# Graph network layer on one Trainium2 core: VectorE prepares masks and one-hots further ahead, TensorE's counts move between the quarters of the products

## The reference

```python
h = jnp.maximum(_layernorm(x), 0.0)                    # x: 6250 x 128
H = _gelu(h @ W1.T + b1)
X_src = H[src]                                         # 200000 edges, dst sorted
W_tar = _gelu(X_src @ WA.T) @ WB.T                     # 4 mixes
cross = X_src[:, :, None] * W_tar[:, None, :]
agg = _gelu(jax.ops.segment_sum(cross, dst, num_segments=num_nodes))
out_edge = jnp.einsum('ehm,em->eh', agg[dst], W_tar)
cnt = jax.ops.segment_sum(ones, dst, num_segments=num_nodes)
agg_node = jax.ops.segment_sum(out_edge, dst, num_segments=num_nodes) / jnp.maximum(cnt, 1.0)[:, None]
out = _gelu(jnp.concatenate([agg_node, H], axis=1)) @ W2.T + b2
return x + out
```

## Time and profile before

| | us |
|---|---|
| time, median of 3 runs | 1252.96 |
| lowest, highest | 1252.32, 1254.63 |
| span of the profiled execution | 1435.7 |
| TensorE busy (matmuls) | 1168.7 |
| VectorE busy | 915.1 |
| GpSimd busy | 849.4 |
| ScalarE busy | 635.0 |

### The profile page before, as it was taken

How to read it: one execution, slowest core, us unless ns; L and a number is a source line. 1 busy time by engine, 2 the same in 40 slices (tenths; PEclk the granted TensorE clock), 3 DMA queues, 4 the chain that set the end, 5 groups by cost and what they waited for, 6 DMA issues and landing times.

```text
span 1435.7 us, 26415 instructions
## 1 busy us (share of the span) xinstructions
PE 1168.7 (81%) x7416; PEld 773.5 (54%) x7416; DVE 915.1 (64%) x2876; ACT 635.0 (44%) x1498; POOL 849.4 (59%) x910
## 2 busy tenths in 40 slices
PE   5948777688887888988788888777888878779888
PEld 3724333366665555656556556555556655456544
DVE  8569987746764677675567767466666755262256
ACT  6976656344342455453455555244554531000023
POOL 5457655556566666666656566655655666656526
PEclk9965555589999999899989999988888999889978
DMA  6345544466555445444545444444444446765523
GB/s 203 130 135 175 171 145 161 142 184 180 167 169 165 134 135 135 126 138 138 144 123 137 121 123 133 140 129 120 127 121 109 125 127 185 176 186 169 174 47 84
DMA packets 100422, 205.73 MB, mean 143 GB/s; under 512 B 29570, under 2 KB 48336, under 8 KB 99611
## 3 DMA queue, kind: packets, MB, share of 16 engines
q1 hardware_dynamic: 74804, 146.92, 33.9%
q0 software_dynamic: 25472, 57.11, 16.2%
HBM read 171.73 MB, written 32.22 MB: 142 GB/s over the span
## 4 chain that ended last, share of the span: by engine, by line
PE 56%; DVE 15%; issue 14%; another core or an unknown queue 5%; DVEq 4%; ACT 3%; POOL 2%; DMA 2%; SPq 0%; ACTq 0%; POOLq 0%
PE ps L1565 23%; PE ps L1546 12%; PE ps L1518 12%; PE ps L1521 3%; DVE big L1195 3%; DVE big L1325 3%; DVE mask L1170 2%; PE ps L1570 2%; DVE q L1204 2%; DVEq L1152 2%; DVE big L1182 2%; POOL q L778 1%; DMA q<-node_table,src_g 1%; PE ps L1614 1%
## 5 line engine op out<-in xcount | busy, mean ns | idle before, releaser
L778 POOL DMA_INDIRECT q<-node_table,src_g x796 | 778.1, 977 | 497.1 <-PE ps L1521 218.6
L1565 PE MATMUL ps<-big,q 128*128 128x298 bf16 (+2 forms) x2940 | 522.7, 319 | 21.1 <-issue 14.2
L894 ACT ACTIVATE hot_b<-iota_b,q 128x128 bf16<-128x128 bf16 x848 | 270.0, 389 | 420.3 <-PE ps L1546 329.4
L1518 PE MATMUL ps<-mask,q 128*128 128x96 f32 x1592 | 291.2, 311 | 107.0 <-DVE mask L1170 67.8
L1565 PEld LDWEIGHTS ps<-big,q 128*128 128x128 bf16 x2940 | 286.5, 105 | 123.7 <-issue 31.1
L1195 DVE TENSOR_TENSOR big<-big,ps 128x294 f32 (+2 forms) x411 | 226.5, 551 | 186.4 <-PE ps L1546 125.6
L1518 PEld LDWEIGHTS ps<-mask,q 128*128 128x128 f32 x1592 | 244.9, 216 | 184.7 <-DVE mask L1170 118.3
L1546 PE MATMUL ps<-q,hot_b 128*128 128x294 bf16 (+2 forms) x848 | 221.7, 349 | 101.0 <-issue 58.4
L1204 DVE TENSOR_SCALAR q<-iota_a,q 128x294 bf16<-128x294 f16 (+2 forms) x848 | 238.0, 324 | 35.4 <-issue 19.8
L1170 DVE TENSOR_TENSOR mask<-eq,q 128x192 f32<-128x192 bf16 x398 | 141.9, 357 | 74.5 <-issue 40.0
L1182 DVE TENSOR_TENSOR big<-big,ps 128x120 f32 x398 | 110.2, 277 | 123.2 <-remote 53.0
(11 more groups left out here) (145 smaller groups left out, 665.7 us busy)
## 6 DMA issues: line engine op xcount, KB each, us to landing
q<-product_parts SPq DMA_DIRECT2D x245, 388.0 KB
product_parts<-big SPq DMA_DIRECT2D x24, 776.0 KB
q<-node_table,src_g POOLq DMA_INDIRECT x796
node_table<-big SPq DMA_DIRECT2D x12, 280.0 KB, 3.0
big<-node_table SPq DMA_DIRECT2D x24, 140.0 KB
own_part<-big SPq DMA_DIRECT2D x12, 256.0 KB, 3.0
out_dram<-q SPq DMA_DIRECT2D x12, 256.0 KB, 2.0
big<-own_part SPq DMA_DIRECT2D x2, 1024.0 KB, 6.2
```

What stands on the lines that cost most here:

```text
L778: pool.indirect_dma_start(out=ring[:, t % R, :], out_offset=None, in_=table, in_offset=bass.IndirectOffsetOnAxis(ap=src_g[:, t:t + 1], axi ...
L894: last = nc.scalar.activation(hot_b[:, b % 2, i, :], iota_b[:, :], ACT.Abs, bias=nkey_b[:, t:t + 1])
L1518: nc.tensor.matmul(o[:, 0:MIX * W], ring[:, s + t, 0:D], mask[:, b, t, :, :], start=(t == 0), stop=(t == G - 1))
L1565: last = nc.tensor.matmul(ps[:, 3 + m, 0:n], c[:, LEAD + P * (MIX * part + m):LEAD + P * (MIX * part + m + 1)], counts[k % 2][:, a, c0:c1] ...
```

## The change

VectorE's order in a slot becomes: register loads, one-hots and masks of the groups of the **next** slot; the additions of this slot's groups, two at a time as soon as a pair is summed; then for each count of this slot the register load and one-hots of the count **two further on**, and the addition of this count itself. Before the first slot it prepares the first slot's groups and the first two counts. TensorE, in stages 1 to 5, no longer runs a slot's counts ahead of the unit but spreads them over the four quarters: one count stands ahead of the last quarter, two ahead of the second and the fourth, three ahead of the second, third and fourth. Stage 0 keeps its order on TensorE. The sizes: ring of gathers 12 tiles (10), ring of VectorE's one-hots 8 tiles (6), product buffers 3 (4), eight registers for group columns (6). The buffer q has 8432 words per partition (8438).

```diff
-R = 10
+R = 12
+AHEAD = 2
-HA = 6
+HA = 8
-CB = 4
+CB = 3
+COUNTS = [c for slot in SLOTS for c in slot.counts]
...
+            def prepare_gathers(slot):
+                for g in slot.gathers:
+                    starts_g[g] = column(regs_g[g % 8], base_g[:, g:g + 1], N - D0)
+                    if g % 2 == 1 and g + 1 < NG:
+                        make_eq(g + 1)
+                    make_mask(g)
+
+            def prepare_counts(number):
+                if number >= CGG:
+                    return
+                c = COUNTS[number]
+                if c.index == 0:
+                    v.wait_ge(keys_ready, KEYED[c.chunk])
+                cell = GROUP0[c.chunk] + c.index
+                starts_c[c.number] = column(regs_c[c.number % 4], base_c[:, cell:cell + 1],
+                                            WIDE[c.chunk] - CWS[c.chunk])
+                hots(c)
+
             make_eq(0)
-            pending_g, pending_c = [], None
-            for slot in SLOTS:
+            pending_g = []
+            prepare_gathers(SLOTS[0])
+            for number in range(AHEAD):
+                prepare_counts(number)
+            for i, slot in enumerate(SLOTS):
...
-                for g in slot.gathers:
-                    starts_g[g] = column(regs_g[g % 6], base_g[:, g:g + 1], N - D0)
-                    if g % 2 == 1 and g + 1 < NG:
-                        make_eq(g + 1)
-                    make_mask(g)
-                    pending_g.append(g)
-                    if g % 2 == 1 and g >= 3:
-                        add_group(pending_g.pop(0))
-                        add_group(pending_g.pop(0))
+                if i + 1 < len(SLOTS):
+                    prepare_gathers(SLOTS[i + 1])
+                pending_g += slot.gathers
+                while len(pending_g) >= 2:
+                    add_group(pending_g.pop(0))
+                    add_group(pending_g.pop(0))
                 for c in slot.counts:
-                    if c.index == 0:
-                        v.wait_ge(keys_ready, KEYED[c.chunk])
-                    cell = GROUP0[c.chunk] + c.index
-                    starts_c[c.number] = column(regs_c[c.number % 4], base_c[:, cell:cell + 1],
-                                                WIDE[c.chunk] - CWS[c.chunk])
-                    hots(c)
-                    if pending_c:
-                        add_counts(pending_c)
-                    pending_c = c
+                    prepare_counts(c.number + AHEAD)
+                    add_counts(c)
...
-                if not slot.counts and pending_c:
-                    add_counts(pending_c)
-                    pending_c = None
```

On TensorE the loop over a count's tiles becomes the function `count(c)`, with the same waits and matmuls, and is called so:

```diff
-                for c in slot.counts:
-                    ...
-                    if s == 0:
+                if s == 0:
+                    for c in slot.counts:
+                        count(c)
                         fill(1 + c.number % 2)
...
-                    pe.wait_ge(cbuf_loaded[u % CB], 16 * (u // CB + 1))
-                    if a == 0:
-                        pe.wait_ge(counts_added, BUILT[s])
                     for m in range(MIX):
+                        for i in share(len(slot.counts), m, MIX):
+                            count(slot.counts[i])
+                        if m == 0:
+                            pe.wait_ge(cbuf_loaded[u % CB], 16 * (u // CB + 1))
+                            if a == 0:
+                                pe.wait_ge(counts_added, BUILT[s])
```

More of the change, by code:

```diff
@@ L217, in gnn_kernel @@
         assert MIX * D0 <= HALF and NT * D <= ACC0 - HALF
-        QW = 3104 + R * ROW + CTT + -(-CTT // 2) + HA * NT * CW // 2 + MIX * SW
+        QW = CB * CROW // 2 + R * ROW + CTT + -(-CTT // 2) + HA * NT * CW // 2 + MIX * SW
         q = sb("q", [P, QW])
@@ L1145, in _ @@
             v.wait_ge(consts, 7)
-            regs_g = [nc.vector.alloc_register(f"start_g{i}") for i in range(6)]
+            regs_g = [nc.vector.alloc_register(f"start_g{i}") for i in range(8)]
             regs_c = [nc.vector.alloc_register(f"start_c{i}") for i in range(4)]
@@ L1288, in _ @@
                 if s == S and slot.at % 2 == 0 and slot.at // 2 < NAB:
-                    i = slot.at // 2
+                    b = slot.at // 2
                     v.wait_ge(counts_added, CGG)
-                    nc.vector.tensor_reduce(most_p[:, i:i + 1], counts[1][:, AB * i:AB * i + AB, :], axis=AX.XY,
+                    nc.vector.tensor_reduce(most_p[:, b:b + 1], counts[1][:, AB * b:AB * b + AB, :], axis=AX.XY,
                                             op=ALU.max).then_inc(most_ready, 1)
@@ L1527, in fill, with count @@
                                  start=True, stop=True)
+            def count(c):
+                n = NT * CWS[c.chunk]
+                if c.number >= 2:
+                    pe.wait_ge(counts_added, c.number - 1)
+                for t in range(c.size):
+                    ct = c.first + t
+                    pe.wait_ge(hot_a_ready, ct + 1)
+                    pe.wait_ge(hot_b_ready, ct // HB + 1)
+                    nc.tensor.matmul(ps[:, 1 + c.number % 2, 0:n], hot_b[:, ct // HB % 2, ct % HB, :],
+                                     hot_a[:, ct % HA, 0:n], start=(t == 0), stop=(t == c.size - 1))\
+                        .then_inc(counted, 1)
             for slot in SLOTS:
@@ L1537, in _ @@
                     sum_group(group_psum(g, 0, SLOT), g % MB, g % EB, G * g % R)
-                for c in slot.counts:
-                    n = NT * CWS[c.chunk]
-                    if c.number >= 2:
-                        pe.wait_ge(counts_added, c.number - 1)
-                    for t in range(c.size):
-                        ct = c.first + t
-                        pe.wait_ge(hot_a_ready, ct + 1)
-                        pe.wait_ge(hot_b_ready, ct // HB + 1)
-                        nc.tensor.matmul(ps[:, 1 + c.number % 2, 0:n], hot_b[:, ct // HB % 2, ct % HB, :],
-                                         hot_a[:, ct % HA, 0:n], start=(t == 0), stop=(t == c.size - 1))\
-                            .then_inc(counted, 1)
-                    if s == 0:
+                if s == 0:
+                    for c in slot.counts:
+                        count(c)
                         fill(1 + c.number % 2)
@@ L1564, in _ @@
                         for part in range(SPL):
-                            last = nc.tensor.matmul(ps[:, 3 + m, 0:n], c[:, LEAD + P * (MIX * part + m):LEAD + P * (MIX * part + m + 1)],
+                            last = nc.tensor.matmul(ps[:, 3 + m, 0:n], cb[:, LEAD + P * (MIX * part + m):LEAD + P * (MIX * part + m + 1)],
                                                     counts[k % 2][:, a, c0:c1], start=(a == 0 and part == 0),
```

4 lines of the change are left out of this document (2 added, 2 removed).

## The result

The changed kernel takes **1240.76 us**, the median of 4 runs (1235.48 to 1241.21), against 1252.74 for the kernel before (4 runs, 1252.32 to 1254.63): a ratio of 0.9883, 95% interval 0.9864 to 0.9901. It is faster by 12 us. The forecast was 1195, a gain of 57; the result is inside the range, near its upper end, and the gain is about a fifth of what was forecast.

A forecast was written before the change was run, and what follows sets the result against it. Bound: TensorE–VectorE hand-over in stages 1 to 4, VectorE in stage 0. Terms 55 + 10 + 5 + 12 - 7 = 75 us, times 0.873 = 65, less 8 for gathers: 57 off 1253, 1195 us; range 1155 to 1245.

The forecast's parts named there:

- The step that failed: All stages: profiled span 1435.7 us against a 1252.96 us median, so every term was scaled to run time by 0.873.
- The gathers' own floor: Stages 2 to 4: 464 gathers at GpSimd's 1.24 us each need 575 us, which took 8 us off the gain.
- the 79 that the forecast kept: Stages 1 to 4: 137 us TensorE idle before counts and gather sums, less 58 for unnamed waits; 70%, 55 us, taken.
- the forecast's signs of being right: Stages 1 to 4: TensorE's idle time before counts falls from 81 to below 45 us, before gather sums 56 to below 35.
- Gathers set the pace: Rival, chance 0.22: stages 2 to 4 end near GpSimd's gather floor plus a hand-over; gain some 25 us, 1228 us.
- Counts between the quarters, one-hots ahead, masks ahead: Stages 1 to 4: shorter TensorE–VectorE hand-over waits, 55 us of profiled span gained, bounds 0 and 79.
- VectorE falls into step: Rival, chance 0.12: in stages 2 to 4 VectorE's added wait at each count paces both engines; 1273 us.
- Additions behind their own count, the added wait: VectorE stands at each count until TensorE has run it; idling there and for masks and pairs gives back 7 us.
- Stage 0, 10 us: VectorE sets stage 0 and idles 30 us; removing part of its waits gains 10 us, bounds 0 and 30.
- Stage 5, 5 us: Stage 5, without counts: masks a slot ahead and one more gather group hide half of TensorE's 10.7 us mask waits.
- Clock, 12 us: Stages 1 to 4: TensorE's granted clock recovers partly as waits close; 12 us gained, bounds 0 and 79.
- Product buffers 3 for 4: Product loads are issued early enough with one buffer less: nothing taken, bounds no cost and 25 us.

The follow-up runs named there:

- e0: The kernel before, no edit, profiled a second time on a chip where it runs near the timed runs: 1256.8 us, span 1255.1.
- e8: The changed kernel, no edit, on a chip where the kernel before takes 1443.25 us: 1435.91 us, ratio 0.9953.
- e4: The changed kernel with every second gather left out, on a chip of the slower kind: 1167.49 us, ratio 0.8128.
- e5: The kernel before with every second gather left out, on a chip of the slower kind: 1219.44 us, ratio 0.8478.
- e9: The changed kernel with every second gather left out, a repetition on a chip of the slower kind: 1171.07 us, ratio 0.8118.
- e10: The kernel before with every second gather left out, a repetition on a chip of the slower kind: 1219.04 us, ratio 0.8448.
- e1: The kernel before with only TensorE's counts spread over the quarters, VectorE's order and sizes as before: 1252.47 us, ratio 0.9996.
- e2: The kernel before with VectorE's new order and the new sizes, TensorE in its old order: 1248.27 us, ratio 0.9972.
- e3: The kernel before with the new sizes alone (gather ring 12, one-hots 8, product buffers 3): 1247.32 us, ratio 0.9948.
- e12: The changed kernel with all gathers, each of 64 rows for 128, on a chip of the faster kind: 1216.82 us, ratio 0.9683.
- e13: The changed kernel with every second gather replaced by ten small memsets on GpSimd, on a chip of the faster kind: 1187.06 us, ratio 0.9446.
- e15: The changed kernel with all gathers, each of 64 rows for 128, repeated on a chip of the faster kind: 1214.37 us, ratio 0.9664.
- e17: The changed kernel with every second gather replaced by twenty small memsets on GpSimd, on a chip of the faster kind: 1208.82 us, ratio 0.9627.

## Why the prediction was wrong

**The step that failed: "Every term below is in microseconds of the profiled span and is turned into run time at the end by 1252.96 / 1435.7 = 0.873."** The 183 us between profile and runs were not spread over everything: between the two profiles of before, 164 of them lie in stages 1 to 4 (888 and 724 us) and none in stage 0 (191 and 191). (The prediction also named its own test, a loss of less than 30 us of span in stages 1 to 4: it is 11.) The prediction took stages 2 to 4 for 729 x 0.873 = 636 us in the runs; e0 shows 592.8. The gathers' own floor, by the prediction's 575 us, was therefore 18 us below the kernel before, not 61, and the hand-over could not be worth more there, whatever was idle before counts and sums. Stages 2 to 4 of after take 582.8, near the floor plus a hand-over, as the rival of the gathers said. By the forecast's terms stages 1 to 4 were to lose (55 + 12 - 7) x 0.873 - 8 = 44 us and lost 11: 33 of the 45 us that are missing between the forecast gain of 57 and the 12 measured.

**What the rows could say.** Of the 137 us of the earlier trace rows, 43.5 and 30.2 are marked "issue", waits for nothing that the profile shows; the named rows come to 29.0 + 4.2 + 24.9 = 58, less than the 79 that the forecast kept. On the short chip the whole idle time before these two groups is 57. That the two numbers are alike proves nothing: in e8 the two groups idle 137 us again, and only 21.2 of them are marked "issue". Only the second profile told what the timed runs have. Two of the forecast's signs of being right look fulfilled beside the first profile (32.3 us before counts and 22.2 before gather sums, for 81 and 56), but e0 has 35.6 and 21.4 without the change.

**The likeliest case and the rival.** The rival "Gathers set the pace" (0.22) holds in its mechanism. Of its signs, one is there: TensorE waits for masks (19.3 us, in e0 20.4) and these for transfers (58.0 us in stages 1 to 4, in e0 25.2). The other is not: GpSimd's pauses for TensorE did not vanish, they are 25.5 us for 26.8, 14.2 of them in stage 1. Its figure of 1228 has no working and is 13 us low.

**Counts between the quarters, one-hots ahead, masks ahead.** The mechanism is right and covered by the gathers: with half of them it is worth 48 to 52 us (e4 and e5, e9 and e10), of which stages 1 to 4 have about 40. The prediction had 55 x 0.873 = 48 for this term. That the two are near is partly luck, since it counted idle time alone and half of the 40 came out of busy time. Alone, TensorE's part gives nothing (e1), because its wait moves to the gather sums; VectorE's part alone brings the step between the engines in stage 4 that the rival "VectorE falls into step" described (e2). With both parts that rival does not occur: VectorE's waits for counts in stages 1 to 4 are 10.8 us, 38.6 in e0.

**Additions behind their own count, the added wait.** Costed at 7 us for masks and pairs. Nothing shows it as a loss; VectorE waits 17.8 us for groups to be summed where e0 has 9.7.

**Stage 0, 10 us.** Wrong: 191 and 189 us. (The 35.6 us of TensorE in the earlier trace rows were read as waits for masks; 32.2 of them are.) VectorE's busy time is 161.7 for 160.6, so the stage stayed VectorE's, and its waits for TensorE were worth little. VectorE's waits in stage 0 of e0:

```profile
DVE q L1204 <- issue: 9.6, 23, 0.7
DVE q L1204 <- PE ps L1546: 5.9, 12, 0.6
```

Of the 15.5 us in the earlier trace rows, only 5.8 named TensorE, and here 5.9. Instead 4 to 6 us came ahead of stage 0 (first gather sum at 92 to 93 us in after, e2 and e8, at 96 to 98 in e0, e1 and e3), where the first masks are built before the first one-hots, a gain I had not listed.

**Stage 5, 5 us.** About right: 3 us between the two profiles, VectorE's waits for gathers there 62.8 to 48.0.

**Clock, 12 us.** Wrong: nothing came back, because nothing was lost. The granted clock of stages 1 to 4 is 0.97 to 0.99 in e0 and 0.97 in after. On the long chip, where it is 0.95 to 0.88 before, e8 has 0.92, 0.93, 0.88 and 0.86. The Trainium skill, page "TensorE: Matmul & The Clock Gate", section "HAM oscillation — how this bites in real kernels", has the clock come back where waits are closed. The rows agree as far as they go: the waits of the long chip were not closed and its clock did not rise, and in e9, on a long chip without them, it is 0.99.

**Product buffers 3 for 4: nothing.** Right. (The bound of 25 us took 6.5 less 4.0 us, which is room, for a cost; the sum does not use it.) TensorE's only wait for a load in stages 1 to 4 of after is one of 7.6 us, in bounds of 10:

```profile
PE ps L1581 <- DMA q<-product_parts: 7.6, 1, 7.6
```

e0 has one of 3.3 us. A cut batch shows no cost either. The Trainium skill, page "Perfetto Trace Analysis", section "Matmul Optimizations", wants matmuls back-to-back; by the rows above the group of all counts has a mean of 325 ns in e0 and 326 in after, so no run here shows a loss.

**Open.** Why TensorE's signals, or its matmuls, are late on the long chips. It is tied to the gathers: with half of them the stalls are gone there (e4, e5, e9, e10). Whether it is the rows moved or the instructions on GpSimd was to be told by e12, e13, e15 and e17, which all came to run on short chips, and so it was not tried where it could be seen.

## What to carry to other kernels

If the span of a profile lies above every timed run, take a second profile before a term is scaled to the runs, and ask stage by stage where the difference lies: here 164 of the 183 us lay in stages 1 to 4. How the waits are named in the first profile doesn't tell which of them the timed runs have. Then lay the floor of each engine that issues at a fixed pace, busy time and pause together, beside the stage's length in run time: an engine that the page calls 68% busy (GpSimd in e0) can be the bound. If such a floor is near, move its work to a stage that another engine bounds, which here gave 20 us for one line, before shortening waits that it covers.

## What the runs showed of the hardware

- A gather of 128 rows occupies GpSimd for 0.96 us with a pause of 0.30 behind it, and one of 64 rows for 0.92: halving the rows saves 4% of it. So the number of gathers, hardly their size, sets the time. The Trainium skill, page "DMA: Bandwidth & Descriptors", section "Anatomy of one DMA — SWDGE (gpsimd) path", puts most of the cost of such a transfer into its completion and calls the making of descriptors small; here what limits is the time on the issuing engine.
- The same kernel takes 1253 to 1256 us on three chips and 1437 and 1443 on two others. On the latter there are stalls in which TensorE's signals reach VectorE, ScalarE and GpSimd together, in the one shown 4.7 us after the record. With half of the gathers the stalls are gone (1219 us for the kernel before on two long chips). The cause is open.
- Small memsets on GpSimd lengthen VectorE's one-hots from 324 to 383 ns and leave its masks as they are (351 ns for 355).
- The busy time of TensorE is not a fixed amount of work: the same matmuls with the same means are 656.3 us of it in e10 and 636.7 in e9, where VectorE prepares them further ahead.
